# Splitting the evictions of the transposes between ScalarE and VectorE, and deferring one small transpose, in a fused attention and mixture-of-LoRA layer

## What is computed

```python
def attn(x, Wq, Wk, Wv, Wo):               # 32 heads of 128, one shared K and V head
    Q = (x @ Wq.T); K = x @ Wk.T; V = x @ Wv.T
    Qr, Kr = rope(Q), rope(K)
    out = sliding_window(Qr, Kr, V)        # window 512, step 256, sigmoid scores
    return out @ Wo.T                      # divided by their sum; windows blended

def ffn(x, base_W, router_W, lora_A, lora_B):
    base = x @ base_W.T
    probs = softmax(x @ router_W.T)        # 8 experts, top 2, renormalised -> w
    mid = (x @ lora_A) * w                 # 8 experts x rank 16 = 128 columns
    return base + 2 * (mid @ lora_B)

x = x + layernorm(attn(layernorm(x)))      # x is (2, 4096, 4096)
x = x + layernorm(ffn(layernorm(x)))
```

## Time and profile before

| what | value |
|---|---|
| executions timed | 2651.79 and 2942.29 us, median 2797.04 us |
| the profiled execution's own time | 2646.34 us |
| its span on the slowest core (core 6) | 2644.8 us |
| spans of the 8 cores | 2621.8 to 2644.8 us |
| TensorE matmul, busy | 1969.3 us (74%) |
| ScalarE, VectorE, GpSimd, busy | 658.9, 579.0, 135.9 us |

### The profile page before, as it was taken

One profiled execution on the slowest core, in us unless ns is written; L12 is line 12 of the kernel. 1 busy time (PEld: TensorE's weight loads), 2 busy tenths in 40 slices (PEclk: granted clock), 3 DMA queues, 4 the chain that ended last, 5 costly groups with the idle time before them and its releaser, 6 DMA issues.

```text
span 2644.8 us, 50094 instructions; the slowest of 8 cores (2621.8 to 2644.8 us)
## 1 busy us (share of the span) xinstructions
PE 1969.3 (74%) x20000; PEld 1692.3 (64%) x20000; DVE 579.0 (22%) x1656; ACT 658.9 (25%) x1159; POOL 135.9 (5%) x194
## 2 busy tenths in 40 slices
PE   1347999999978777777999999712212999999900
PEld 0237999999956556556888888612212888888800
DVE  2431222222233333444000000243340000000055
ACT  2660101111154444453111111143331011111122
POOL 1000000000000000000000000001011000010000
PEclk9999999999986888987999999955555999999955
DMA  9821555665520000000665665422123465566346
GB/s 207 199 96 33 65 65 65 76 81 69 65 33 2 2 2 2 2 2 2 62 85 65 83 78 65 71 56 48 48 64 43 57 89 77 67 80 86 50 155 210
DMA packets 228592, 179.01 MB, mean 68 GB/s; under 512 B 18960, under 2 KB 222736, under 8 KB 222736
## 3 DMA queue, kind: packets, MB, share of 16 engines
q0 software_dynamic: 217568, 113.35, 34.4%
q1 hardware_dynamic: 10800, 62.45, 6.7%
HBM read 263.97 MB, written 25.17 MB: 109 GB/s over the span
## 4 chain that ended last, share of the span: by engine, by line
PE 67%; issue 9%; DMA 9%; DVE 8%; ACT 6%; POOL 1%; DVEq 1%; SPq 0%; POOLq 0%; ACTq 0%
PE ps_all L813 17%; PE ps_all L669 17%; PE ps_all L454 17%; PE ps_all L556 7%; DMA xstage<-x_ext 3%; DVE bn L264 3%; DMA x1re<-x_scratch 2%; ACT sig L518 2%; DMA xre<-x_ext 2%; PE ps_all L504 2%; DVE bl L592 1%; PE ps_all L622 1%; ACT xt_stage L283 1%; PE ps_all L693 1%; DVE outstage L848 1%
## 5 line engine op out<-in xcount | busy, mean ns | idle before, releaser
L813 PE MATMUL ps_all<-slab,ln2T 128*128 128x256 bf16 x4096 | 462.9, 273 | 27.5 <-DMA brider<-b_all 27.5
L454 PE MATMUL ps_all<-slab,ln1T_own 128*128 128x256 bf16 x4096 | 467.9, 273 | 0.6 <-ACT krT L380 0.6
L669 PE MATMUL ps_all<-slab,attn_T 128*128 128x256 bf16 x4096 | 448.8, 273 | 1.1 <-ACT attn_T L630 1.1
L813 PEld LDWEIGHTS ps_all<-slab,ln2T 128*128 128x128 bf16 x4096 | 401.6, 98 | 74.9 <-issue 27.7
L669 PEld LDWEIGHTS ps_all<-slab,attn_T 128*128 128x128 bf16 x4096 | 401.4, 98 | 48.4 <-issue 1.2
L454 PEld LDWEIGHTS ps_all<-slab,ln1T_own 128*128 128x128 bf16 x4096 | 395.4, 98 | 44.3 <-issue 0.8
L518 ACT ACTIVATE sig<-ps_all,kbias_s 128x512 bf16<-128x512 f32 x384 | 226.0, 719 | 242.7 <-PE ps_all L504 242.4
L556 PE MATMUL ps_all<-v_sb,sig 128*128 128x128 bf16 x2048 | 234.0, 243 | 48.3 <-DVE bl L592 43.7
L556 PEld LDWEIGHTS ps_all<-v_sb,sig 128*128 128x128 bf16 x2048 | 221.2, 123 | 59.6 <-issue 59.5
L566 PE MATMUL ps_all<-onesc,sig 128*128 128x1 bf16 x2048 | 228.8, 188 | 0.0
L566 PEld LDWEIGHTS ps_all<-onesc,sig 128*128 128x128 bf16 x2048 | 192.1, 100 | 0.0
(11 more groups left out here) (90 smaller groups left out, 1509.2 us busy)
## 6 DMA issues: line engine op xcount, KB each, us to landing
slab<-wqT POOLq DMA_DIRECT2D x16, 2048.0 KB, 18.9
slab<-woT POOLq DMA_DIRECT2D x16, 2048.0 KB, 18.1
slab<-baseT POOLq DMA_DIRECT2D x16, 2048.0 KB, 14.5
xstage<-x_ext SPq DMA_DIRECT2D x12, 2048.0 KB, 15.2
out<-outstage SPq DMA_DIRECT2D x8, 2048.0 KB, 8.9
xre<-x_ext POOLq DMA_DIRECT2D x8, 1024.0 KB, 8.0
x_scratch<-x1b SPq DMA_DIRECT2D x8, 1024.0 KB, 3.9
x1re<-x_scratch SPq DMA_DIRECT2D x8, 1024.0 KB, 10.5
```

Source lines behind the costliest of these rows:

```text
L454: return e.matmul(reg, ln1T_own[:, d, t * 128:(t + 1) * 128], slabs[par][:, d, :], start=(d == 0), stop=(d == 31))
L669: return e.matmul(reg, attn_T[:, d, t * 128:(t + 1) * 128], slabs[par][:, d, :], start=(d == 0), stop=(d == 31))
L813: return e.matmul(reg, ln2T[:, d, t * 128:(t + 1) * 128], slabs[par][:, d, :], start=(d == 0), stop=False)
```

## The change

Two things. First, `emit_transpose_tile` gets a mode "alt", used in stages A and E: the even groups of a tile are evicted by ScalarE as before, the odd ones by VectorE (`tensor_copy`), which counts on a new semaphore `s_tpe2`. Since the banks alternate too, one bank is now always emptied by ScalarE and the other by VectorE. Whoever waited for `s_tpe` now waits for both. Second, the transpose of `midg` and its eviction leave `emit_router`; `emit_mgT` appends them one tile later, behind the next tile's router, and the copy to `router_sb` also waits for the previous `midg`.

```diff
@@ emit_transpose_tile
-            if evac_eng == "scalar":
+            eng = ("scalar" if (g & 1) == 0 else "vector") if evac_eng == "alt" else evac_eng
+            if eng == "scalar":
                 def fe(e, bank=bank, g=g):
                     return e.activation(out=dst_view_fn(g), in_=bank[:, :], func=AF.Copy)
             else:
                 def fe(e, bank=bank, g=g):
                     return e.tensor_copy(dst_view_fn(g), bank[:, :])
-            P.op(evac_eng, fe, waits=[(s_tp, c_tp)], inc=s_tpe)
-            tpb_ring.release_last((s_tpe, s_tpe.n))
-        return s_tpe.n
+            sem = s_tpe if eng == "scalar" else s_tpe2
+            P.op(eng, fe, waits=[(s_tp, c_tp)], inc=sem)
+            tpb_ring.release_last((sem, sem.n))
+        return [(s_tpe, s_tpe.n), (s_tpe2, s_tpe2.n)]
@@ emit_a (dpost_s3 likewise)
-                                   extra_apply_waits=[(s_tpe, s_tpe.n)])
+                                   extra_apply_waits=[(s_tpe, s_tpe.n), (s_tpe2, s_tpe2.n)])
-        emit_transpose_tile(xt_stage[:, :], dvf, src_waits=[(s_apply, c_ap)])
-        a_evac_counts[ti] = s_tpe.n
+        a_evac_counts[ti] = emit_transpose_tile(xt_stage[:, :], dvf,
+                                                src_waits=[(s_apply, c_ap)],
+                                                evac_eng="alt")
@@ emit_router
         P.op("scalar", lambda e: e.activation(out=router_sb[:, 0:128], in_=ps[4][:, 0:128], func=AF.Copy),
-             waits=[(s_mmm, c_m)], inc=s_mev)
+             waits=[(s_mmm, c_m), (s_pool, last_midg[0])], inc=s_mev)
...
-        c_mg = s_pool.n
+        last_midg[0] = s_pool.n
+        pend_mg[0] = (t, mp, s_pool.n)
+
+    def emit_mgT(job):
+        t, mp, c_mg = job
         tb, tw = mg_ring.acquire()
@@ the loop of E
         if t >= 2:
+            prev_mg = pend_mg[0]
             dpost_s3(t - 2)
+            if prev_mg is not None:
+                emit_mgT(prev_mg)
         if t < NT:
             dpost_s1(t)
+    emit_mgT(pend_mg[0])
```

More of the change, by code:

```diff
@@ L211, in build_program @@
     s_tpe   = P.sem("s_tpe")
+    s_tpe2  = P.sem("s_tpe2")
     s_kvmm  = P.sem("s_kvmm")
@@ L353, in emit_b0 @@
             P.op("tensor", f,
-                 waits=(kvw + [(s_wkv, WKV_N), (s_tpe, a_evac_counts[ti])]) if d == 0 else ())
+                 waits=(kvw + [(s_wkv, WKV_N)] + a_evac_counts[ti]) if d == 0 else ())
             def f2(e, d=d, ti=ti, vb=vb):
@@ L388, in build_program @@
         emit_b0(ti)
-    B0_DONE = s_tpe.n
+    B0_DONE = [(s_tpe, s_tpe.n), (s_tpe2, s_tpe2.n)]
     B0_KV = s_kvmm.n
@@ L401, in build_program @@
     q_ring = Ring([ps[0], ps[1], ps[2], ps[3]],
-                  init_conds=[(s_tpe, B0_DONE)])
-    qtp_ring = Ring([ps[4], ps[5]], init_conds=[(s_tpe, B0_DONE)])
+                  init_conds=list(B0_DONE))
+    qtp_ring = Ring([ps[4], ps[5]], init_conds=list(B0_DONE))
     qm_free = {0: [], 1: []}
@@ L438, in emit_qtp @@
         if first_qev[0]:
-            wev.append((s_tpe, B0_DONE))
+            wev.extend(B0_DONE)
             first_qev[0] = False
@@ L688, in build_program @@
     mgT_counts = {}
+    pend_mg = [None]
+    last_midg = [0]
     m_free_l = [m_free]
@@ L695, in emit_router @@
             P.op("tensor", f,
-                 waits=(list(m_free_l[0]) + [(s_fw2, FW2_N), (s_tpe, ln2t_counts[t])]) if d == 0 else ())
+                 waits=(list(m_free_l[0]) + [(s_fw2, FW2_N)] + list(ln2t_counts[t])) if d == 0 else ())
             def f2(e, d=d, t=t):
@@ L788, in dvf @@
             return ln2T[:, 4 * g:4 * g + 4, t * 128:(t + 1) * 128]
-        emit_transpose_tile(proj[:, t, :], dvf, src_waits=[(s_apply, c_ap2)])
-        ln2t_counts[t] = s_tpe.n
+        ln2t_counts[t] = emit_transpose_tile(proj[:, t, :], dvf,
+                                             src_waits=[(s_apply, c_ap2)],
+                                             evac_eng="alt")
         emit_router(t)
@@ L795, in build_program @@
         if t >= 2:
+            prev_mg = pend_mg[0]
             dpost_s3(t - 2)
+            if prev_mg is not None:
+                emit_mgT(prev_mg)
         if t < NT:
             dpost_s1(t)
+    emit_mgT(pend_mg[0])
     D_DONE = (s_x1w[0].n, s_x1w[1].n)
-    E_DONE = s_tpe.n
+    E_DONE = [(s_tpe, s_tpe.n), (s_tpe2, s_tpe2.n)]
     y_ring = Ring([ps[2], ps[3]], init_conds=[(s_pev, D_MM)])
```

## The result

The changed kernel takes 2700.82 us (median of 9 executions) against 2650.25 us before (8 executions). The ratio is 1.0194, with a 95% interval of 1.0176 to 1.0212: the change made the kernel slower by some 51 us. The ratio leaves out executions in which the cores of one die run slower (in one of 2960.6 us after the change the cores of one die had a granted clock of 0.78 to 0.80, the others 0.88 to 0.89; 2942.29 and 2840.49 us before are of that size), so the median of 2797.04 us that stood ahead of the forecast is no yardstick for it.

A forecast was written before the change was run, and what follows sets the result against it. It took A to be paced by loads, then by ScalarE's applies and evictions with statistics hidden, and E by one closed chain a tile. 2646.34 + 54.3 (A) + 3.4 (E) = 2704 us, range 2686 to 2722.

The forecast's parts named there:

- Part 1: Stage A: the next tile's statistics wait on VectorE behind the odd evictions, 17.59 us a tile; +54.3 us.
- rival 3: Stage A: loads of two or three early tiles come late by about 4 us; 2716 us; chance 0.08.
- rival 4: Stage A: statistics slip in front of the odd evictions and still overlap; 2650 us; chance 0.01.
- The loop of the banks: Transposes: each bank's fill, empty and refill sets the pace, 1.52 us a pair; the odd loop becomes 0.11 longer.
- rival 1: Stages A and E: two engines empty twice as fast; A +25, E -16, result 2655 us; chance 0.07.
- Part 2: Stage E: the split evictions add 0.43 us a tile to the closed chain; +3.4 us.
- Part 3: Stage E: the deferred transpose takes away TensorE's 75.0 us wait for `midg`, costed at nothing.
- Rival 2: Stage E: the wait for `midg` was on the path and its 75.0 us come back; 2629 us; chance 0.04.
- 40 us a tile: Stage E: one tile is one closed chain of 40 us (321.0 by 8 tiles).

## Why the prediction was right or wrong, point by point

**The time.** 2704 us were forecast, with a range of 2686 to 2722; 2700.82 were measured. Against the kernel before, that is +1.94% by the ratio, where I had forecast +2.2% and put the line between "slower" and "within 2%" at the forecast itself. The measured value lies just under that line, and the interval of 1.76 to 2.12% has it inside, so the measurement doesn't tell the side. That 2704 came so near is in part luck. The change was put at +57.7 us and is some +51; but the sum started from the profiled execution's 2646.34, which is 3.9 us below the 2650.25 measured, and that hid half of the error. In the +57.7 itself two errors of opposite sign meet, the deferral (8 us too high) and B0 (2 too low).

**Part 1, statistics behind the odd evictions.** Right in mechanism and size. Forecast +54.3 us with 17.59 us a tile and the copy at 680 ns; measured +53.2, 17.47 and 692 ns. No tile but the first waited for its load, on any core, so rival 3 is out; and no statistics slipped in front of the copies (rival 4). The runs with a single copy show that it is the place in the list: +10 us with the copy early, +50 with it late; turning the list round takes 38 us back. The Trainium skill, VectorE: DVE Perf Modes, section on the TRN2 errata, gives an estimate of 658 ns for this copy (120 cycles and 512 columns at 0.96 GHz); the trace has 692, and that decides.

**The loop of the banks.** Right. The even bank's loop stayed at 1.52 us, the odd one's became 1.64 where I had 1.63, and four banks bring the evictions to one each 0.5 us. The advice of the Trainium skill, TensorEngine Tiling (Array Packing), section PSUM Bottleneck, to evacuate with both engines did not help here, since the evacuating engine was not what bound: rival 1 would have made E 16 us shorter, and E with the split alone became 2.8 us longer.

**Part 2, the split in E.** Right: +3.4 forecast, +2.8 to +3.4 measured.

**Part 3, the deferral at nothing.** Wrong. My step was: "Behind it TensorE could only do the first two groups of the next tile, whose next step, ScalarE's eviction, waits behind an apply some 20 us later." That holds for tiles 1 to 6 (first to last add unchanged, 261.6 against 261.9), not for tile 7. The last pass of the loop calls neither `dpost_s2` nor `dpost_s1`, so no apply stands ahead of tile 7's evictions; there the wait for `midg` was on the path, and 8 us come back. I read a steady tile and took it for all; the loop's last pass was never looked at. My 40 us a tile hid it too: that was all of E by 8 tiles, while from one add to the next it was 37.4 us (261.9 by 7), and the rest belongs to the first and last passes. Rival 2, which had all 75 us on the path, is wrong by nearly the same step: a ninth of it was on the path.

**What no term covered.** B0 became 2.1 us longer, in every run with copies on VectorE in A and in none without (64.5 to 64.9 against 62.2 to 63.2). I had written that outside A and E the change touches "only waits that are long satisfied", and priced them at nothing there. The last section has what the rows say of them. With B0's 2, Part 1's -1 and the deferral's -8, the sum of the forecast goes from +57.7 to some +51, which is what the medians show.

**Which core ends last.** It changed from core 6 to core 2 between the two profiles, as I had said it might, but this shows nothing: in the executions of the changed kernel five different cores ended last. In A after the change all eight cores take the same time from their own first load.

## What to carry to other kernels

Before work is moved to an idle engine, look at what stands behind it in that engine's in-order list: 3 us of copies a tile cost 6 us in each late tile of A and 53 over the stage here, because the next tile's statistics stood behind the last of them. Where the loop of fill, empty and refill of two banks sets the pace, as here, a second engine to empty them gains nothing; more banks do. And a wait that is hidden in the steady state may be bare in the last pass of a loop: price first and last passes by themselves.

## What the runs showed of the hardware that was not expected

One more wait on a TensorE instruction went with a longer gap before it, though what it waits for is long done. The first K matmul of each tile in B0 waits for `s_tpe2` besides its other semaphores; TensorE's list in B0 differs in nothing else. From the last transposing matmul of one tile to the first K matmul of the next, before and after (core 2 of both):

```profile
203.79 0.22 PE L377 MATMUL ps_all<-identB,km 128*128 128x128 bf16 x1
204.31 0.22 PE L351 MATMUL ps_all<-wkT_s,ln1T_own 128*128 128x128 bf16 x1 [0.30 <-issue]
```

```profile
254.12 0.22 PE L381 MATMUL ps_all<-identB,km 128*128 128x128 bf16 x1
254.77 0.22 PE L355 MATMUL ps_all<-wkT_s,ln1T_own 128*128 128x128 bf16 x1 [0.43 <-ACT krT L384]
```

0.52 us became 0.65. At most of the eleven such places of core 2 it is 0.39 before and 0.49 to 0.59 after; the eleven together make 1.4 of B0's 2.1 us, and the rest was not traced. Most gaps are 0.49 to 0.59 also in the four runs with VectorE copies in A alone, with one copy a tile no less than with four, and 0.38 to 0.42 in the runs with the deferral alone and with the split in E alone, where this wait is not there. That the wait itself is the cause was not tried by changing nothing else.
